# A new order of the work on all engines, one whole masked sum instead of two halves, and one bound operation instead of two

## The reference, cut to what matters

```python
x = x + _L0_conv_ref(_gn(x), ...)          # a 3x3 convolution with a weight of its own for each of 3136 positions
x = x + _L1_conv_ref(_gn(x), ...)          # the part that the change touches, below

# _L1_conv_ref, batch 32, n = 56*56 = 3136 points, c = 32 channels, K = 16
p = pts / max(norm(pts, axis=1), 1e-12)
dist = sq + (-2.0 * einsum('bnc,bmc->bnm', p, p)) + swapaxes(sq, 1, 2)
_, nn_idx = top_k(-dist, K)                 # the 16 nearest points of each point
nbr = pts[bidx, nn_idx]
e, e_n = pts @ W_emb + b_emb, nbr @ W_emb + b_emb
logits = leaky_relu(concat([e, e_n]) @ W_att + b_att, 0.1)
attn = softmax(logits, axis=2)              # over the 16 neighbours
agg = sum(nbr * attn, axis=2)
y = concat([pts, agg]) @ W_conv + b_conv    # then batch norm over all points, relu, + pts
```

## Time and profile before

| what | us |
|---|---|
| time, median of 3 runs | 11595.12 (11594.07 to 11595.4) |
| time of the profiled execution | 11598.23 |
| its span | 11596.5 |
| DVE busy | 9543.5 (82%) |
| PE busy | 8956.0 (77%) |
| ACT busy | 8100.1 (70%) |
| POOL busy | 4929.9 (43%) |

### The profile page before, as it was taken

How to read it: one execution, slowest core, us unless ns; L and a number is a source line. 1 busy time by engine, 2 the same in 40 slices (tenths; PEclk the granted TensorE clock), 3 DMA queues, 4 the chain that set the end, 5 groups by cost and what they waited for, 6 DMA issues and landing times. The chain is left out here.

```text
span 11596.5 us, 331616 instructions
## 1 busy us (share of the span) xinstructions
PE 8956.0 (77%) x114762; PEld 6411.4 (55%) x114762; DVE 9543.5 (82%) x24722; ACT 8100.1 (70%) x10793; POOL 4929.9 (43%) x3642
## 2 busy tenths in 40 slices
PE   4885578788787888878788887888887878878875
PEld 3664355555555555555555555555555555555553
DVE  1001599999989999999999898989999999989997
ACT  3332377777777777777777777777777777767765
POOL 1221044444444444444444444444444444444442
PEclk9887889999999999999999999999999999989998
DMA  8666867777777777777777777777776777767766
GB/s 203 174 179 173 263 140 153 153 153 151 148 150 150 151 154 148 147 149 152 152 148 154 150 153 145 155 150 151 154 150 140 151 148 146 154 137 156 156 126 208
DMA packets 460414, 1818.08 MB, mean 157 GB/s; under 512 B 166244, under 2 KB 174052, under 8 KB 442084
## 3 DMA queue, kind: packets, MB, share of 16 engines
q0 software_dynamic: 252672, 1380.97, 58.6%
q1 hardware_dynamic: 206020, 414.62, 13.4%
HBM read 404.97 MB, written 105.90 MB: 44 GB/s over the span
## 5 line engine op out<-in xcount | busy, mean ns | idle before, releaser
L900 POOL TENSOR_SCALAR masked<-steeps,minus_own 128x1568 f32<-128x1568 f32 x1600 | 2498.6, 1562 | 4345.1 <-DVE rest L1257 3622.8
L1163 DVE MAX8 found<-scores 128x8 f32<-128x224 f32 x11200 | 3493.5, 374 | 501.7 <-ACT scores L1066 473.0
L1093 ACT ACTIVATE turned_sb<-psum 128x512 f32<-128x512 f32 (+1 forms) x5600 | 2894.7, 555 | 513.1 <-PE psum L978 419.6
L1066 ACT ACTIVATE scores<-psum 128x1568 f32<-128x1568 f32 x1600 | 2361.6, 1476 | 1098.9 <-PE psum L957 835.8
L980 PE MATMUL psum<-ident_a,masked 128*128 128x128 f32 x19200 | 2719.2, 286 | 72.0 <-issue 67.9
L980 PEld LDWEIGHTS psum<-ident_a,masked 128*128 128x128 f32 x19200 | 2415.2, 197 | 519.3 <-issue 518.2
L903 POOL DMA_DIRECT2D masked<-shares_a x1600 | 2221.1, 1388 | 973.9 <-POOL masked L900 909.8
L978 PE MATMUL psum<-ident_a,masked 128*128 128x128 f32 (+1 forms) x10400 | 1769.3, 285 | 756.0 <-ACT turned_sb L1093 721.7
L1078 ACT ACTIVATE masked<-masked,minus_top 128x3136 f32<-128x3136 f32 x800 | 2337.2, 2922 | 0.0
L978 PEld LDWEIGHTS psum<-ident_a,masked 128*128 128x128 f32 (+1 forms) x10400 | 1107.7, 140 | 1512.5 <-issue 1439.3
L953 PE MATMUL psum<-points 32*128 32x392 f32 x12800 | 1580.4, 564 | 25.9 <-DMA rows<-table 16.7
(11 more groups left out here) (148 smaller groups left out, 6610.9 us busy)
## 6 DMA issues: line engine op xcount, KB each, us to landing
masked<-shares_a POOLq DMA_DIRECT2D x1600, 784.0 KB, 7.2
w_in<-in_L_conv_weight_dram POOLq DMA_DIRECT2D x392, 144.0 KB, 3.4
w_in<-in_L_conv_weight_dram SPq DMA_DIRECT2D x392, 144.0 KB, 3.6
points<-unit SPq DMA_DIRECT2D x128, 392.0 KB
shares_a<-share SPq DMA_DIRECT2D x32, 1568.0 KB
steeps<-steep SPq DMA_DIRECT2D x64, 784.0 KB, 6.7
windows<-xg SPq DMA_DIRECT2D x42, 928.0 KB, 14.0
xg<-padded SPq DMA_DIRECT2D x16, 812.0 KB, 18.3
```

The source lines that it names most:

```text
L900: nc.gpsimd.tensor_scalar(masked[:, t.ring, cols], steeps[:, cols], -NEVER, minus_own[:, t.half, at:at + 1], ALU.min, ALU.max).then_inc(cl ...
L1066: nc.scalar.activation(scores[:, t.par, quad * QUAD:(quad + 1) * QUAD].rearrange("p (a b) -> p a b", b=SCH), ps[:, 0:PER * BANK].rearrange ...
L1093: nc.scalar.activation(turned_sb[0:high, t.par, g * GROUP:g * GROUP + width // P, :].rearrange("p a b -> p (a b)"), ps[0:high, bank:bank + ...
L1163: n = step(nc.vector.max(found[:, t.par, c, :], scores[:, t.par, c * PART:(c + 1) * PART]))
```

## The change

On DVE the masked sum becomes one operation over 3136 columns and moves from the next step to the place directly behind the bar of the same step; one operation on the bound is left; the doubt is asked for behind five of the seven maxima of the next tile instead of two, so that two are left behind it. On PE the second score products go ahead of the count's product, and the seven turned groups of a tile are now split in four (lag 2) and three (lag 3). On ACT the copies follow, the whole turned groups 2 to 6 stand behind the exponential, and the per-batch `minus_own` is made five tiles ahead of the batch's end. On POOL the low half's clamp waits for the masked sum and the high half's for the count, both for the coming tile. On SP both halves of the next slopes are loaded in one step.

The bound itself changes in its arithmetic: before, two bounds were made from the sixteenth best value with a relative and an absolute margin; now the bar uses the sixteenth best value itself and the count uses it less an absolute margin of 2.0e12.

```diff
-NORM_LAG = 5
+NORM_LAG = 4
@@ POOL
             def body(tile):
-                here, coming = tile(0), tile(-1)
-                if here:
-                    clamp_high(here, tile(1))
+                coming = tile(-1)
                 if coming:
-                    clamp_low(coming, tile(RING - 1), here)
+                    clamp_low(coming, tile(RING - 1), tile(1))
+                    clamp_high(coming, tile(0))
@@ PE
-                if older:
-                    turn(older, 5)
                 if coming:
                     score(coming, 0)
-                if older:
-                    turn(older, 6)
-                if past:
-                    turn(past, 0)
-                    turn(past, 1)
-                if tile(Y_LAG) and tile(Y_LAG).ends_group():
-                    convolve_1x1(tile(Y_LAG))
-                if here:
-                    add_doubts(here)
-                if past:
-                    turn(past, 2)
-                if older:
-                    spread_inverse(older)
-                if coming:
-                    score(coming, 1)
-                if past:
-                    turn(past, 3)
                 if older:
                     aggregate(older)
                 if past:
                     turn(past, 4)
+                    turn(past, 5)
+                    turn(past, 6)
+                if fresh:
+                    turn(fresh, 0)
+                    turn(fresh, 1)
+                if tile(Y_LAG) and tile(Y_LAG).ends_group():
+                    convolve_1x1(tile(Y_LAG))
+                if coming:
+                    score(coming, 1)
+                if fresh:
+                    turn(fresh, 2)
+                    turn(fresh, 3)
+                if here:
+                    add_doubts(here)
+                if past:
+                    spread_inverse(past)
@@ DVE
-            def mask_low(t):
+            def mask(t):
                 gate(dve, slope_in[t.par], t.same_par(32, 32), dve_passed)
                 gate(dve, barred, t.count(1, 1), dve_passed)
-                m = masked[:, t.ring, 0:HALF]
-                nc.vector.tensor_tensor_reduce(m, m, scores[:, t.par, 0:HALF], -1.0, -NEVER, ALU.add, ALU.min,
-                                               low_top[:, t.par:t.par + 1]).then_inc(low_masked, 1)
-            def mask_high(t):
-                gate(dve, low_masked, t.count(1, 1), dve_passed)
-                m = masked[:, t.ring, HALF:N]
-                nc.vector.tensor_tensor_reduce(m, m, scores[:, t.par, HALF:N], -1.0, low_top[:, t.par:t.par + 1],
-                                               ALU.add, ALU.min, minus_top[:, t.ring:t.ring + 1]).then_inc(masked_ready, 1)
+                m = masked[:, t.ring, :]
+                nc.vector.tensor_tensor_reduce(m, m, scores[:, t.par, :], -1.0, -NEVER, ALU.add, ALU.min,
+                                               minus_top[:, t.ring:t.ring + 1]).then_inc(masked_ready, 1)
-            def lower_bound(n):
+            def set_bound(n):
                 dve.wait_ge(chain, n)
-                return step(nc.vector.scalar_tensor_tensor(bound_low[:], over[:], last, margin[:], ALU.mult, ALU.subtract))
-            def set_bound(n):
+                return step(nc.vector.tensor_scalar(bound[:], last, MARGIN, None, ALU.subtract))
-                dve.wait_ge(chain, n)
-                return step(nc.vector.scalar_tensor_tensor(bound[:], under[:], last, bound_low[:], ALU.mult, ALU.min))
             def body(tile):
                 if here:
                     n = search(here, 1)
-                if passed:
-                    mask_low(passed)
-                if here:
                     n = top_first(here, n)
-                if passed:
-                    mask_high(passed)
-                if here:
                     n = drop_first(here, n)
 ...
                 if coming:
-                    search(coming, 0, 0, 2)
+                    search(coming, 0, 0, 5)
                 if here:
                     ask_doubts(here)
                 if coming:
-                    search(coming, 0, 2)
+                    search(coming, 0, 5)
                 if here:
                     settle_doubts(here)
                     bar(here)
+                    mask(here)
```

More of the change, by code:

```diff
@@ L706, in attend @@
     NEVER = -3.0e38
-    MARGIN = 1.0e12
-    TINY = 2.0 ** -22
+    MARGIN = 2.0e12
+    NEXT_OWN = 20
     OWN = TILES
@@ L729, in attend @@
         weight8 = enter(nc.sbuf_tensor("weight8", [P, PARTS, H8], FP32))
[L730 removed]
         best = enter(nc.sbuf_tensor("best", [P, NEIGHBOURS], FP32))
[L732 to L736 removed]
+        bound = enter(nc.sbuf_tensor("bound", [P, 1], FP32))
         above = enter(nc.sbuf_tensor("above", [P, 1], FP32))
@@ L871, in body @@
                 here = tile(0)
-                if ends_batch(here):
-                    next_steep(here, 1)
                 if ends_batch(tile(-1)):
-                    next_steep(tile(-1), 0)
+                    for k in range(2):
+                        next_steep(tile(-1), k)
                 if here and here.c == 7 and not (isinstance(here.i, int) and here.at > ALL - TILES):
@@ L903, in clamp, with clamp_low @@
                 pool.dma_start(masked[:, t.ring, cols], shares[:, t.half, cols], accum_op=ALU.add).then_inc(slope_in[t.par], 16)
-            def clamp_high(t, passed):
-                if t.c == 0:
-                    gate(pool, steep_in[1], t.batch(16, 16), pool_passed)
-                if passed:
-                    gate(pool, barred, passed.count(1, 1), pool_passed)
-                clamp(t, 1)
-            def clamp_low(t, used, beside):
+            def clamp_low(t, used, passed):
                 if t.c == 0:
@@ L1135, in _ @@
             nc.vector.memset(weight8[:], 1.0).then_inc(chain, 1)
-            for k in range(2):
-                nc.vector.memset(over[:, k:k + 1], 1.0 + (k + 1) * TINY).then_inc(chain, 1)
-                nc.vector.memset(under[:, k:k + 1], 1.0 - (k + 1) * TINY).then_inc(chain, 1)
-                nc.vector.memset(margin[:, k:k + 1], (k + 1) * MARGIN).then_inc(chain, 1)
             dve.wait_ge(const_loaded, 16 * (6 + PER))
-            dve.wait_ge(chain, 9)
+            dve.wait_ge(chain, 3)
             nc.vector.memset(weight8[:, :, H8 - 1:H8], float(NEIGHBOURS)).then_inc(chain, 1)
             nc.vector.tensor_scalar(spread[:], spread[:], emb_bias[:, 0:1], None, ALU.mult).then_inc(spread_ready, 1)
-            dve.wait_ge(chain, 10)
+            dve.wait_ge(chain, 4)
             dve.sem_clear(chain)
             steps = [0]
+            last = best[:, NEIGHBOURS - 1:NEIGHBOURS]
             def step(instruction):
@@ L1183, in settle_doubts @@
                     nc.vector.tensor_scalar(s, s, -1.0, None, ALU.mult).then_inc(exact, 1)
-                    nc.vector.memset(bound[:], 1.0e38).then_inc(exact, 1)
+                    nc.vector.memset(last, 1.0e38).then_inc(exact, 1)
                 with dve.Else():
@@ L1222, in normalise @@
                                         ALU.mult).then_inc(agg_ready, 1)
-            last = best[:, NEIGHBOURS - 1:NEIGHBOURS]
             def found_of(t):
```

77 lines of the change are left out of this document (35 added, 42 removed).

## The result

The changed kernel is slower: 12070.6 us (12055.98 to 12082.77, 4 runs) against 11594.6, ratio 1.041, 95% interval 1.040 to 1.043. Its profiled execution has a span of 12054.0 us. The forecast was 11,520.

What follows compares the result with a forecast made beforehand. A ring through DVE, PE and ACT made ordinary steps 11.91 us; DVE alone would bound them at 11.93. Steps +14, loads -90, stage end -5: -81, kept as -75, took 11595.1 to 11520, range 11,390 to 11,680.

Steps and rivals of the forecast that it cites:

- the way from the doubt to the bar: On DVE, the sequencer waits for the doubt's integer, loads it, branches and clears: 1.38 us, 0.69 of it new idle time.
- the slope wait: DVE's wait for a slope DMA at a batch element's load: from 6.4 to 3.5 us, -90 us over 31 loads.
- the bar beside POOL's issue: DVE's bar starts 0.4 us behind POOL's second DMA issue: the bar keeps 1.82 us, POOL gives way.
- The bar at 5924.25: One DVE bar before the change, 0.25 us late even behind five maxima, read as some 1.8 us from doubt to bar.
- the long way in every step: Rival at the branch over the exact path: 0.42 us more a step, 336 us, time 11,860; chance 8%.
- The ring: DVE's count, PE's count product, score products, ACT's copy, DVE's search, bound, count again: DVE waits 0.58 us a step for ACT.
- DVE's other parts: In DVE's step: count to next search 3.69 us, five maxima 1.48, bar to masked sum 2.04, whole sum 3.34.
- The rival of the bar held by POOL's issue: Rival on the port shared by DVE and POOL: the bar blocks, 0.48 us a step, +384 us, time 11,900; chance 3%.
- The question's wait for PE's count product: DVE asks for the doubt at 5.2 us of the step, PE's product is done at about 4.3: no wait.

Runs made afterwards that it cites:

- the low half small: The changed kernel, but the slope DMA of each tile's low half moves an eighth of its columns, leaving out part of the slope term: 11580.0 us.
- every byte moved: The changed kernel, nothing left out, with POOL clamping both halves in succession and issuing both slope DMAs only when the doubt's integer is there: 11720.1 us.
- the question came earlier: The changed kernel with the doubt asked for behind two of the seven maxima again instead of five, so that five stand behind it: 11783.6 us.
- the way was gone: The changed kernel without the register's load, the branch and the exact path; the doubt is counted and asked for but not acted upon: 11186.3 us.

## Why the prediction was wrong

**The step that failed** is this one: "I take 1.38 on average, bounds 1.34 and 1.8", for the way from the doubt to the bar. It measured 1.90, above even the upper bound. On 800 steps the 0.52 are 416 us of the 476; with this term right the forecast of 11,520 becomes 11,936. The kernels whose load falls outside the slope transfer ran in 11580.0 (the low half small) and in 11720.1 (every byte moved).

The reasoning behind it failed in one point. The last step of the stage and the ordinary steps had their load outside the slope transfers. I took the distance as the sequencer's own and constant, and looked only at what covers it. But the change also moved POOL: the low half's DMA, issued behind the count before, is issued at the step's start now, and its transfer covers the load. The prediction worked out when the transfers start for the slope wait and for the bar beside POOL's issue, and never laid them beside the load. The trace of the kernel before had the answer, at the very place that the prediction names. The bar at 5924.25 was late because of the load ahead of it:

```profile
L1174 DVEq TENSOR_LOAD <-doubts x1: 804/804/804, 5922.7 to 5922.7; - x1
```

POOL had begun to issue a slope DMA at 5921.24, and the engines moved 223 GB/s from 5922.60 to 5923.50. Five maxima cover 1.53 us of a way, and with this load it took 1.85.

A slower rival had the right place and nearly the right price (the long way in every step, 11,860), at 8%, and for the wrong reason, a fetch behind the branch. The Trainium skill (Runtime: NRT & Kernel Launch, Instruction fetch mechanics) says that a taken branch to code outside the fetched pages stalls for a fetch. That is not what acted here, since the same branch took the short way in both kernels in which the transfer was away from the load.

**What held.** The ring was read rightly: with the second products ahead of the count's, the waits for ACT go, alone (0.977) as in the change. DVE's other parts came out within 0.02 us each. At the loads of a batch element, DVE's waits for slope DMAs fell from 161.2 us to 58.4 in the stretch, from 6.2 a load (26 loads) to 2.4 (24 loads); 3.5 were forecast. The rival of the bar held by POOL's issue is out. In the changed kernel the two hardly meet, since the bar comes late: in the step shown POOL issues from 6020.28 to 6021.18, and the bar starts at 6021.22. But in the kernel with the low half small they meet in most steps (697 of 800 bars start while an issue is under way, with a median of 1.86 us), as in the two rows of its timeline above. The issue starts 0.35 us ahead, the bar still begins when its queue lets it and takes 1.85 us, and it is the issue that is stretched, to 2.29 us from 0.88. The Trainium skill (SBUF — State Buffer, Who interferes with whom) says that whichever starts first holds the shared ports for its whole instruction; this trace does not agree.

**What was too optimistic.** The question's wait for PE's count product was costed at nothing. It was 77.6 us in the stretch in the change, 279.1 when the question came earlier, 222.8 when the way was gone. I worked out the product's place in an ordinary step only, at PE's full clock. In the change 59 of the 78 us stand in steps without a 1x1 convolution, and 53 of the 78 stand in steps in which PE's granted clock was below its full level shortly before the question. The step behind the one shown is of this kind. PE's clock in it:

```profile
6030.00:6031.00 1.00, 1.00 (x6) 1.00 (x6) 0.96 (x6) 1.00 (x1) 0.39 (x1) 0.50 0.56 113
```

The clock of 0.50 is the level of 1.2 GHz. Eight of the transposes (L972) took 1.92 us there instead of 1.06, the count's product came at 6031.84, 5.23 us into the step instead of 4.26, and DVE's question waited 0.20 us. Where the question came earlier or the way was gone, the steps with a convolution had most of the wait (182 of 306 us and 139 of 224, all of DVE's idle time at the question counted).

**Left open.** What the register's load shares with the slope transfer, so that it takes three times as long, no run separates. In the kernel before, 65 of the 800 loads also had twelve engines or more at the slopes 0.3 us behind their start, and their median is 0.752 us: behind five maxima they cost little there. Of the 134 us between 11,936 and 12,070 the waits for PE are some 100 by an estimate (77.6 us in 611 steps, for 800); the rest no experiment took apart.

## What to carry to other kernels

A register load that a branch depends on is a memory access of its own. Here an SBUF-to-SBUF transfer beside it made it three times as long, and a load of other data at the same rate did not. When a change moves DMA issues, lay their transfers beside every such load, not only beside the consumers of the data, and look up the load's own duration where an odd delay shows in the trace before. Cut the ring that bounds the step first and alone: here two moved calls on PE and ACT were worth 2.3% alone, and with the rest of the change the kernel was 4.1% slower. And work that stands between a producer and its consumer may be the cover or may free a buffer: before moving or merging it, ask what it hid and whom its first half released.

## What the runs showed of the hardware that was not expected

- DVE's register load from SBUF has a median of 0.305 us in the kernel before and of 0.90 us in the changed one, where it falls into a 784 KB slope transfer (220 to 238 GB/s in the step shown); emptying the other transfer of the step left it at 0.899. Beside the batch element's data at 226 GB/s it took 0.308.
- A wait of DVE that its sequencer handles ahead of the load delays the load, although only maxima in DVE's queue needed it: 2.83 us from doubt to bar instead of 1.90 in the steps shown.
- The masked sum on 3136 columns takes 3.42 us, two halves 1.78 and 1.85: merging saves 0.14 us from start to start, less than the 0.28 that the bar's result costs when the sum stands directly behind it.
- A bar of DVE that starts 0.35 us behind the start of a DMA issue of POOL is not held (1.85 us); the issue is stretched from 0.88 to 2.29 us.
